# Flamingo block on one core: the first residual sum moved from VectorE to GpSimd, its gate folded into the cosines

## The reference

```python
def _L0_xattn_ref(visual_features, text_features, Wv, bv, Wt, bt):
    v = jnp.einsum('bsd,hd->bsh', visual_features, Wv) + bv
    t = jnp.einsum('bsd,hd->bsh', text_features, Wt) + bt
    dots = jnp.einsum('bih,bjh->bij', v, t)
    vn = jnp.linalg.norm(v, axis=-1)
    tn = jnp.linalg.norm(t, axis=-1)
    denom = jnp.maximum(vn[:, :, None] * tn[:, None, :], EPS)
    return dots / denom
...
x = x + jnp.tanh(g_xattn[0]) * _L0_xattn_ref(_layernorm(x, axis=-1), ctx_768, ...)
x = x + jnp.tanh(g_ffn[0]) * _L0_ffn_ref(_layernorm(x, axis=-1), ...)
x = x + jnp.tanh(g_xattn[1]) * _L1_xattn_ref(_layernorm(x, axis=-1), ctx_768, ...)
x = x + jnp.tanh(g_ffn[1]) * _L1_ffn_ref(_layernorm(x, axis=-1), ...)
```

## Time and profile before

| | |
|---|---|
| runs shown | 318.55, 321.72, 322.47 us, median 321.72 |
| profiled execution | 321.48 us, of which the span from the first to the last instruction is 319.6 us |
| granted TensorE clock over the span | 0.984 |
| busy: PE, PEld, DVE, ACT, POOL | 293.5, 238.7, 241.1, 230.0, 163.0 us |
| first block (to about 112 us), attention rounds (to about 270 us), the rest | all start times below are us from the start of the span |

### The profile page before, as it was taken

The page is one execution under the profiler, slowest core; times in us unless marked ns, Lnnn a source line. Parts: engine busy times, 40 slices in busy tenths (PEclk is TensorE's granted clock), DMA queues, the critical chain, the costliest instruction groups (busy, mean ns, idle before and its releaser), DMA issues.

```text
span 319.6 us, 7710 instructions
## 1 busy us (share of the span) xinstructions
PE 293.5 (92%) x2602; PEld 238.7 (75%) x2602; DVE 241.1 (75%) x722; ACT 230.0 (72%) x773; POOL 163.0 (51%) x231
## 2 busy tenths in 40 slices
PE   7788999999999869999999999999999898887595
PEld 6567768686766658998998988988989786553375
DVE  3798999999785446776877878778778776648755
ACT  2777696869899678878778878778778765239170
POOL 2124617342542135358779697885857568254000
PEclk9999999999999999999999999999999999979879
DMA  5741010002020000000000000000000000000004
GB/s 147 191 125 27 1 27 1 1 2 66 7 62 3 0 0 2 2 1 3 2 1 2 2 3 3 0 2 4 1 2 3 2 0 3 0 2 1 0 8 126
DMA packets 11478, 6.67 MB, mean 21 GB/s; under 512 B 3824, under 2 KB 10992, under 8 KB 11440
## 3 DMA queue, kind: packets, MB, share of 16 engines
q1 hardware_dynamic: 10560, 5.99, 6.8%
q10 hardware_dynamic: 880, 0.20, 0.3%
HBM read 5.14 MB, written 1.05 MB: 19 GB/s over the span
## 4 chain that ended last, share of the span: by engine, by line
PE 73%; DVE 11%; ACT 7%; issue 3%; DMA 3%; SPq 2%; POOL 1%; DVEq 0%; ACTq 0%
PE psum L1041 15%; PE psum L1168 10%; PE psum L1465 10%; PE psum L1479 9%; PE psum L1045 7%; PE psum L1047 6%; PE psum L1046 6%; PE psum L1056 3%; DVE hgm L2071 2%; DMA KT<-in_L_ffn_w_down 2%; PE psum L1558 2%; DVE nmx L1937 2%; SPq L387 2%; DVE work L1931 1%; DVE KT L2077 1%
## 5 line engine op out<-in xcount | busy, mean ns | idle before, releaser
L985 ACT ACTIVATE work<-psum,nmx 128x129 f32<-128x129 f32 x256 | 83.5, 419 | 22.8 <-DVE nmx L1937 22.8
L574 POOL TENSOR_TENSOR work<-work,rden 128x512 f32<-128x512 f32 x64 | 66.8, 1044 | 45.1 <-DVE rden L1950 44.6
L1041 PE MATMUL psum<-ident,work 128*128 128x128 f32 (+2 forms) x376 | 58.4, 281 | 2.9 <-DVE work L1931 2.6
L1937 DVE TENSOR_REDUCE nmx<-psum 128x4 f32<-128x516 f32 x64 | 41.6, 690 | 25.4 <-PE psum L1168 25.2
L985 ACT ACTIVATION_READ_ACCUMULATOR work<-psum,nmx 128x1 f32 x256 | 58.4, 228 | 0.0
L1045 PE MATMUL psum<-split 97*128 97x512 f32 (+1 forms) x128 | 52.0, 406 | 1.5 <-issue 0.8
L1041 PEld LDWEIGHTS psum<-ident,work 128*128 128x128 f32 (+2 forms) x376 | 41.3, 142 | 12.0 <-issue 3.4
L1931 DVE COPY work<-psum 128x512 f32<-128x512 f32 x64 | 43.9, 686 | 5.3 <-PE psum L1041 1.7
L1047 PE MATMUL psum<-split 97*128 97x512 f32 (+1 forms) x128 | 43.2, 338 | 0.0
L1046 PE MATMUL psum<-split 97*128 97x512 f32 (+1 forms) x128 | 43.2, 337 | 0.0
L1479 PE MATMUL psum<-work 128*128 128x128 f32 x256 | 39.0, 275 | 1.0 <-ACT work L965 1.0
(11 more groups left out here) (195 smaller groups left out, 537.0 us busy)
## 6 DMA issues: line engine op xcount, KB each, us to landing
KT<-in_L_xattn_Wkv SPq DMA_DIRECT2D x2, 384.0 KB, 4.8
X<-in_x SPq DMA_DIRECT2D x1, 768.0 KB, 5.8
out_x<-X SPq DMA_DIRECT2D x3, 256.0 KB, 2.3
work<-in_ctx SPq DMA_DIRECT2D x3, 192.0 KB, 2.5
work<-in_L_xattn_Wq SPq DMA_DIRECT2D x1, 512.0 KB, 3.5
work<-in_L_xattn_Wout SPq DMA_DIRECT2D x1, 512.0 KB, 4.0
X<-in_x SPq DMA_DIRECT2D x1, 256.0 KB, 3.3
KT<-in_L_ffn_w_gate SPq DMA_DIRECT2D x1, 256.0 KB, 5.9
```

The costliest lines, as they stand in the source:

```text
L574: pool.tensor_tensor(sx_[:, :, 0:S], sx_[:, :, 0:S], bcast(rden[n % 2][:, :], S), ALU.mult).then_inc(p_ready.sem, 1)
L985: ins = act.activation(Sx[n % 4][:, j, :], psum[:, here, (j // 2) * K1:(j // 2 + 1) * K1], ACT.Exp, bias=nmx[n % 2][:, j:j + 1], accum_out ...
L1041: return pe.transpose(dst, src, ident[0:m, 0:m])
L1937: dve.tensor_reduce(nmx[n % 2][:, :].rearrange("p (c a) -> p c a", a=2), sim, AX_X, ALU.max, negate=True).then_inc(max_done.sem, 1)
```

## The change

The tanh of the gate, tg[:, 0:1], is now a factor of the cosines: where VectorE multiplied ctxT by the dot products in PSUM with a tensor_tensor, it now does ctxT times gate times dot products with one scalar_tensor_tensor. The sum into X is now a plain tensor_tensor add on GpSimd. It signals step 3 of cos_step as before, and waits for the same two semaphores. In GpSimd's list it stands behind masked_context(2) for group 0, behind norm_power(1, 1) for group 1, behind masked_context(3) for group 2, and behind third_rstd(0) for group 3. The four calls are gone from VectorE's list. The wait for the gate (group 0 alone) moves from the sum to the cosines.

```diff
--- before.py
+++ after.py
@@ -510,6 +510,12 @@
                     pool.wait_ge(cos_step.sem, cos_step.at(1, s - 1))
                 pool.tensor_tensor(rn[:, k, :], n2[:, k, :], half[:, 0:G], ALU.pow).then_inc(rnorm.sem, 1)
 
+            def first_residual(s):
+                xg = X[:, s * G:(s + 1) * G, :]
+                pool.wait_ge(cos_step.sem, cos_step.at(2, s))
+                pool.wait_ge(xn1_ready.sem, xn1_ready.at(1, s))
+                pool.tensor_tensor(xg, xg, cosw, ALU.add).then_inc(cos_step.sem, 1)
+
             def second_rstd(s):
                 pool.wait_ge(stats2.sem, stats2.at(2 * G, s))
                 rsqrt(mv2[:, :, 1], ve2[:, :], rstd2[:, :], 1.0, LN_EPS, ve2_done, rstd2_done, s)
@@ -532,10 +538,12 @@
             norm_power(0, 1)
             first_rstd(2)
             masked_context(2)
+            first_residual(0)
             second_rstd(0)
             first_rstd(3)
             norm_power(1, 0)
             norm_power(1, 1)
+            first_residual(1)
             second_rstd(1)
             norm_power(2, 0)
             h_scaled(0, 0)
@@ -544,6 +552,7 @@
             h_scaled(0, 2)
             h_scaled(0, 3)
             masked_context(3)
+            first_residual(2)
             second_rstd(2)
             norm_power(3, 0)
             norm_power(3, 1)
@@ -552,6 +561,7 @@
             h_scaled(1, 2)
             h_scaled(1, 3)
             third_rstd(0)
+            first_residual(3)
             second_rstd(3)
             h_scaled(2, 0)
             h_scaled(2, 1)
@@ -1698,16 +1708,10 @@
             def cosines(s):
                 dve.wait_ge(cos_step.sem, cos_step.at(1, s))
                 dve.wait_ge(dots_done.sem, dots_done.at(1, s))
-                dve.tensor_tensor(ctxT, ctxT, bank[2], ALU.mult).then_inc(cos_step.sem, 1)
-
-            def first_residual(s):
-                xg = X[:, s * G:(s + 1) * G, :]
                 if s == 0:
                     dve.wait_ge(setup_a.sem, setup_a.at(2))
-                dve.wait_ge(cos_step.sem, cos_step.at(2, s))
-                dve.wait_ge(xn1_ready.sem, xn1_ready.at(1, s))
-                dve.scalar_tensor_tensor(out=xg, in0=cosw, scalar=tg[:, 0:1], in1=xg, op0=ALU.mult,
-                                         op1=ALU.add).then_inc(cos_step.sem, 1)
+                dve.scalar_tensor_tensor(out=ctxT, in0=ctxT, scalar=tg[:, 0:1], in1=bank[2], op0=ALU.mult,
+                                         op1=ALU.mult).then_inc(cos_step.sem, 1)
 
             def second_stats(s):
                 dve.wait_ge(cos_step.sem, cos_step.at(3, s))
@@ -1830,7 +1834,6 @@
             inverse_norms(0)
             first_stats(2)
             cosines(0)
-            first_residual(0)
             first_norm(2)
             second_stats(0)
             down_scale()
@@ -1844,7 +1847,6 @@
             quantised_rows(0)
             inverse_norms(1)
             cosines(1)
-            first_residual(1)
             second_stats(1)
             h_product(0, 0)
             h_max(0, 0)
@@ -1864,7 +1866,6 @@
             context_low(2)
             inverse_norms(2)
             cosines(2)
-            first_residual(2)
             second_stats(2)
             second_residual(0)
             h_product(1, 0)
@@ -1884,7 +1885,6 @@
             row_scale(2)
             cosines(3)
             quantised_rows(2)
-            first_residual(3)
             third_stats(0)
             second_stats(3)
             second_residual(1)
```

## The result

The changed kernel takes 329.01 us (median of 4 runs, 328.46 to 330.16) against 321.43 of the kernel before (4 runs, 318.55 to 322.47): 7.6 us or 2.4% slower by the medians, and the ratio of the means is 1.0254 with a 95% interval of 1.0192 to 1.0315. The forecast was 327.0 with a range of 323.5 to 330.0; I had put the chance of more than 2% slower at 0.24. The profiled execution took 328.69 us with a span of 326.9.

A forecast was written before the change was run, and what follows sets the result against it. TensorE and VectorE were taken as both full where the sums lie, with GpSimd on group 0's path; 3.4 + 0.4 + 1.7 = +5.5 us on the profiled 321.48 gave 327.0, range 323.5 to 330.0.

The forecast's parts named there:

- text_proj(1): TensorE's text projection of group 1, held because ctx_evac(1) waits for GpSimd's sum: 3.6 us later.
- group 0 at spread_norms(1): Group 0's overlapping delays through ctx_evac(1) and VectorE's statistics, less a 0.2 us earlier wait: +3.4 us on TensorE.
- groups 1 and 2: VectorE's statistics wait for GpSimd's sum after the cosines, 0.5 us more per group; TensorE at gate_up(1, 1): +0.4 us.
- group 3: Sum behind third_rstd(0) delays second_stats(3) by 2.1 us, partly absorbed by idle time; TensorE at gate_up(2, 1): +1.7 us.
- first scores: TensorE's first score matmuls, behind all four groups: 5.5 us later, with rounds and tail unchanged in length.
- The mechanism: Group 0's sum waits behind masked_context(2)'s load; VectorE's freed 2.7 us become waits, and TensorE recovers nothing from 76 us on.
- the granted clock is 1.00 of full speed there ... and little can be won or lost by it: From 20 to 112 us, where the sums lie: TensorE stays at its upper level of 2.4 GHz, so no clock term.
- dearer additions: Rival: GpSimd's add stretched to 1.33 us by VectorE's work, idle times absorb nothing; +7.7 us, 329.2; chance 0.20.
- The price of the add: GpSimd's 128x512 float32 add taken as 1.04 us from a multiply with one input broadcast; upper end 1.33.
- Only the buffer of group 0: Rival: hidden TensorE slack before gate_up(1, 1) and gate_up(2, 1) fades later terms; +3.4 to +3.8 us, about 325.2; chance 0.14.
- The other side: Rival: VectorE alone is the bound and GpSimd hides the sums, so 2.7 us come off: 318.8; chance 0.06.

The follow-up runs named there:

- own_buf: Changed kernel, but ScalarE writes the context of group 1 into a free part of hbuf, so ctx_evac(1) need not wait for GpSimd's sum; 327.08 us.
- order0: Changed kernel with first_residual(0) moved ahead of masked_context(2) in GpSimd's list; 324.08 us.
- g0_vector: Changed kernel with the sum of group 0 back on VectorE as a plain add, groups 1 to 3 still on GpSimd; 325.38 us.
- fill_half: Changed kernel with 19 small matmuls on TensorE between kv(10) and text_proj(1), to fill its idle time; 326.59 us.
- fold_only: Changed kernel's arithmetic with the gate folded into the cosines, but all four sums on VectorE as plain adds; 320.75 us, ratio 1.0027 to the kernel before.
- early_0_3: Changed kernel with sums 0 and 3 on GpSimd ahead of masked_context(2) and third_rstd(0), sums 1 and 2 plain adds on VectorE; 323.09 us, ratio 1.0084.
- order3: Changed kernel with first_residual(3) moved ahead of third_rstd(0) in GpSimd's list; 329.96 us.
- order3_stats: As order3, and in VectorE's list third_stats(0) moved ahead of quantised_rows(2); 329.12 us.
- g0_only: Changed kernel with only the sum of group 0 on GpSimd, sums 1 to 3 plain adds on VectorE; 327.1 us.
- fill_gap: Changed kernel with 38 small matmuls on TensorE between kv(10) and text_proj(1), which ran past the idle time; 331.95 us.
- fold_warm: fold_only with 11 instead of 3 small matmuls on TensorE behind text_proj(0); 319.37 us against 321.04 for the kernel before.

## Why the prediction was right, and which term was off

Term by term, counted at TensorE:

| step | forecast | measured |
|---|---|---|
| text_proj(1) | +3.6 | +3.6 |
| group 0 at spread_norms(1) | +3.4 | +6.3, with the clock kept up +3.5 |
| groups 1 and 2 | +0.4 | +0.4 |
| group 3 | +1.7 | +1.2; +1.7 in own_buf, order0 and g0_vector |
| first scores | +5.5 | +7.9, with the clock kept up +5.2 |

- **The mechanism held.** The sum stood behind the load, ScalarE's reuse of ctxT carried the wait to TensorE, and the stream of kv units was no cover (order0 and own_buf). VectorE's freed time went into waits, and TensorE made nothing good from 76 us on.
- **The term of group 0 was mis-sized, and the step that failed is "the granted clock is 1.00 of full speed there ... and little can be won or lost by it".** I carried the 3.6 us through the stretch as if it kept its length. But the change itself makes the idle time (4.54 us where 0.94 had been), and TensorE came out of it at 1.2 GHz. fill_half takes that away and lands 0.3 us from my sum at the first scores. Part of that closeness is luck, since group 3 was 0.5 cheaper there than forecast. The measured time is in the range, but the range had no term for the clock; its upper end came from dearer additions and the scatter.
- **The price of the add was low.** I took 1.04 from a multiply of the same shape with one input broadcast; the add with two full inputs took 1.26 to 1.28, all four times, near my upper end of 1.33. The trace of before had the right row, and I overlooked it (groups by line): a multiply of the same shape on GpSimd with both inputs full, near 290 us.
```profile
L663 POOL TENSOR_TENSOR KT<-KT,work 128x512 f32<-128x512 f32 x3 | 3.9, 1285 | 3.7 <-ACT KT L1024 3.7
```
  That the 3.6 us at text_proj(1) came out all the same is luck: the add was 0.2 us dearer, but counted from the first spread_norms the masking began 0.1 us earlier, and the add began 0.04 us before the end of its last row, where I had allowed 0.08 behind it. Against the same plain add on VectorE (0.69 in fold_only) the ratio is 1.84. I had written that the trace doesn't agree with the factor of two from the Trainium skill, "GPSIMD Engine Reference", "Engine selection"; I had compared unlike operations, and like with like it nearly does. Nor does the spread from 0.70 to 0.985 us show contention with two SBUF inputs, as I wrote: beside the instruction of 0.985 VectorE ran L1774, a tensor_scalar of one tensor, which had started 0.07 us earlier.
- **The rivals.** "Dearer additions" gave 329.2, which is almost the measured time, by another cause: the adds were dearer by 0.2 us by their own form, but not stretched by VectorE, since it was idle, and the idle times did absorb. So the 0.24 for more than 2% rested mainly on the wrong mechanism. "Only the buffer of group 0" fails, since groups 1 and 2 cost 0.4 us and group 3 another 1.2 to 1.7. "The other side" fails in early_0_3: even with no wait on GpSimd's list, the sums are no gain.

## What to carry to other kernels

An engine that is half idle on average may be the one that the path runs through at the very place of a move, so read what its list waits for there, and who reuses the buffer that the moved step reads. When an edit makes TensorE wait for microseconds, count the matmuls behind the wait at half clock as well, even if the trace of before shows full clock throughout. Price a moved elementwise operation by a row with the same number of full inputs, from any part of the trace, and look for single-input operations of VectorE beside it.

## What the runs showed of the hardware that I had not expected

- After 4.5 to 4.6 us without a matmul TensorE ran at 1.2 GHz for 6.4 to 7.7 us of its work, in all four profiles with that wait (changed, order3, order3_stats, g0_only); from text_proj(1) to spread_norms(1) it took 8.9 to 9.5 us instead of 6.25, so 2.7 to 3.3 us each. After about 2.1 us it fell in two profiles (own_buf, early_0_3) and stayed up in one (order0). Near 10 us it fell after 1.8 us in fill_gap and 1.9 in fold_only and stayed up after 2.06 in early_0_3 and 1.74 in the kernel before, and in fold_warm it fell after 1.34 near 20 us, so the length of the idle time alone doesn't decide it. The runs' times go with their mean clocks: of the 17 runs of before beside fold_warm, those at 0.989 or more took 318.8 to 320.2 us but for one of 322.8, those at 0.979 or less 321.0 to 324.3. How much of the scatter comes from such falls wasn't shown.
- GpSimd's add (1.27 us) holds tensor_scalars of VectorE from SBUF to SBUF. In order3 one of four takes 1.31 us, to the end of the add, and the others 0.27, so 0.86 becomes 1.90; in order0 the 2.61 instead of 1.12 is the add and masked_context's multiply, one after the other. The add doesn't hold the statistics (1.14 us beside it and alone), and it isn't slowed in these rows. Holding goes the other way as well: in the kernel before, at 98.18, a one-input operation of GpSimd takes 0.98 us instead of 0.70 where VectorE's had started 0.07 us earlier. The Trainium skill, "GPSIMD Engine Reference", "Key points", names contention with VectorE's instructions in a two-port mode or with two SBUF inputs. No row names the mode of the tensor_scalars, so the first half isn't shown here, though the held ones have one tensor as input; the second half wasn't tried.
- On GpSimd an add of 128x512 with two full inputs takes 1.27 us, a multiply of that kind 1.29 and a multiply with a broadcast input 1.04, while at 128x256 an add with full inputs and a multiply with a broadcast one take 0.74 and 0.73. Why the forms part only at the larger width wasn't tried.
